# Four-part expert weights issued ahead of the next pair's queries and mask rows on SyncE's DMA queue

## The reference, cut to what matters

```
x = x + einsum('bct,bcd->bdt', x, w0[cond])      # layer 0: a 64x64 matrix chosen per sequence
x = x + attention(x, Wq, Wk, Wv, Wo, k_blocks, v_blocks, block_tables, kv_lens)
                                                 # layer 1: 8 heads, 4 kv groups, window of 256 keys
x = x + einsum('bsi,bio->bso', x, W[id]) + b[id] # layer 2: one of 16 experts, 512x512, per sequence
x = x + x W3^T + scaling * (x A^T) B^T           # layer 3: dense, with one of 8 adapters of rank 16
```

## Time and profile before

| | us |
|---|---|
| median of 3 runs (lowest, highest) | 1223.86 (1220.88, 1235.68) |
| the profiled execution's own time | 1219.34 |
| span of the profiled execution | 1217.5 |
| mean granted clock of TensorE | 0.955 of full |
| busy: TensorE / VectorE / GpSimd / ScalarE | 1075.5 / 652.0 / 529.0 / 485.2 |
| moved by DMA | 187.90 MB, mean 154 GB/s |

### The profile page before, as it was taken

The page is one execution under the profiler, slowest core; times in us unless marked ns, Lnnn a source line. Parts: engine busy times, 40 slices in busy tenths (PEclk is TensorE's granted clock), DMA queues, the critical chain, the costliest instruction groups (busy, mean ns, idle before and its releaser), DMA issues.

```text
span 1217.5 us, 23807 instructions
## 1 busy us (share of the span) xinstructions
PE 1075.5 (88%) x6602; PEld 726.5 (60%) x6602; DVE 652.0 (54%) x1924; ACT 485.2 (40%) x1295; POOL 529.0 (43%) x598
## 2 busy tenths in 40 slices
PE   1999899999626898999999999999999999999997
PEld 0766677887413565556666565665566655656555
DVE  5789886337713454545545455554555555454542
ACT  3344343224413343444444444344444444444440
POOL 2344443324554545545445445444454445444400
PEclk9999998779857898999999999999999999999998
DMA  3334343334234554665555665556565566554530
GB/s 104 107 119 141 118 149 104 107 115 154 104 110 149 170 170 142 189 200 193 161 165 178 188 208 167 167 176 179 193 192 170 159 192 200 186 163 159 175 135 18
DMA packets 90376, 187.90 MB, mean 154 GB/s; under 512 B 30386, under 2 KB 39218, under 8 KB 82150
## 3 DMA queue, kind: packets, MB, share of 16 engines
q1 hardware_dynamic: 59622, 143.35, 34.7%
q0 software_dynamic: 30720, 44.15, 13.9%
HBM read 186.83 MB, written 33.56 MB: 181 GB/s over the span
## 4 chain that ended last, share of the span: by engine, by line
PE 55%; issue 4%; DVE 4%; ACT 2%; DMA 1%; POOL 0%; ACTq 0%; DVEq 0%; POOLq 0%
PE bank L85 18%; PE bank L1246 9%; PE bank L1216 8%; PE bank L1195 7%; PE bank L1203 5%; PE bank L1182 4%; PE bank L1172 2%; DVE SM L1081 2%; ACT PT L1003 1%; DMA KV<-kv_scratch,idxs 1%; PE bank L1235 1%; DVE XAL L1075 1%; DVE XAM L1124 0%; DVE XAH L1129 0%; DMA KV<-in_pool,idxs 0%
## 5 line engine op out<-in xcount | busy, mean ns | idle before, releaser
L940 POOL DMA_INDIRECT KV<-kv_scratch,idxs x192 | 190.5, 992 | 287.5 <-DMA KV<-in_pool,idxs 248.5
L1081 DVE CUSTOM_DVE_ANT_0 SM<-bank,FM 128x336 f32<-128x336 f32 x256 | 130.1, 508 | 253.6 <-PE bank L1195 198.5
L930 POOL DMA_INDIRECT KV<-in_pool,idxs x192 | 192.5, 1003 | 136.7 <-PE bank L1216 68.8
L1003 ACT ACTIVATE PT<-bank 112x384 f32<-112x384 f32 x256 | 112.3, 489 | 263.8 <-PE bank L1203 188.3
L1012 ACT ACTIVATE PR<-SM,nb 128x336 f32<-128x336 f32 x256 | 145.1, 576 | 0.6 <-DVE nb L1085 0.6
L1216 PE MATMUL bank<-PT,KV 112*64 112x128 f32 x1536 | 111.4, 280 | 28.7 <-ACT PT L1003 24.3
L1216 PEld LDWEIGHTS bank<-PT,KV 112*64 112x64 f32 x1536 | 84.3, 137 | 78.6 <-issue 44.6
L1003 ACT ACTIVATE KT<-bank 128x336 f32<-128x336 f32 x128 | 57.7, 451 | 175.3 <-PE bank L1182 168.5
L1246 PE MATMUL bank<-W,XT 128*64 128x512 f32 x512 | 123.7, 604 | 0.9 <-issue 0.7
L85 PE MATMUL bank<-wqh,XTH 128*128 128x512 f32 x256 | 107.0, 418 | 12.2 <-DVE XTL L470 11.8
L673 POOL TENSOR_TENSOR RT<-RT,SW 128x384 f32<-128x384 f32 x32 | 32.4, 1012 | 188.4 <-DVE SW L479 188.4
(11 more groups left out here) (166 smaller groups left out, 1946.2 us busy)
## 6 DMA issues: line engine op xcount, KB each, us to landing
W<-in_w SPq DMA_DIRECT2D x64, 1024.0 KB
FM<-mask SPq DMA_DIRECT2D x64, 168.0 KB
X<-in_x SPq DMA_DIRECT2D x32, 256.0 KB, 2.9
x_scratch<-X SPq DMA_DIRECT2D x32, 256.0 KB, 2.0
kv_scratch<-KVR SPq DMA_DIRECT2D x32, 256.0 KB, 2.6
qt_scratch<-QT SPq DMA_DIRECT2D x32, 256.0 KB, 2.9
QB<-qt_scratch SPq DMA_DIRECT2D x32, 256.0 KB
XB<-x_scratch SPq DMA_DIRECT2D x32, 256.0 KB
```

The source lines that it names most:

```text
L930: pool.indirect_dma_start(out=KV[k][:, c, :], out_offset=None, in_=t["pool"], in_offset=bass.IndirectOffsetOnAxis(ap=idxs[k][:, c:c + 1], ...
L940: pool.indirect_dma_start(out=KV[k][:, c, :], out_offset=None, in_=kv_d, in_offset=bass.IndirectOffsetOnAxis(ap=idxs[k][:, NCH + c:NCH + c ...
L1003: return nc.scalar.activation(dst, src, ACT.Copy)
L1081: v.tensor_tensor_reduce(out=SM[u % 2][:, :], in0=bank[u % 2][:, 0:SPAN], in1=FM[k][:, :], scale=1.0, scalar=-3e38, op0=ALU.add, op1=ALU.m ...
```

## The change

The function `weights` of SyncE now takes a list of parts and a step. Each part is a quarter of a sequence's expert weights (128 partitions x 512 values, 256 KB) with a DMA of its own, so a pair has eight DMAs of 256 KB where it had two of 1 MB, and TensorE waits for 64 counts of the semaphore instead of 16. Ahead of each two parts SyncE waits for a score step of pair p. All weights of pair p are issued behind the XB1 load of body p, and the queries and mask rows of pair p+1 behind them all. Another semaphore, `s_pass_sp`, is only counted up.

```diff
-                    def weights(b):
-                        e = sp.value_load(eid[0:1, bass.ds(p * 2 + b, 1)], min_val=0, max_val=E - 1)
-                        wait(sp, s_l2, p - 1)
-                        sp.dma_start(W2[pr.par][b][:, :], w2_v[bass.ds(e, 1)]).then_inc(s_w2in[pr.par][b], 16)
-
+                    def weights(b, parts, step):
+                        if parts[0] == 0:
+                            regs[b] = sp.value_load(eid[0:1, bass.ds(p * 2 + b, 1)], min_val=0, max_val=E - 1)
+                            wait_all(sp, s_pass_sp, (s_l2, p - 1))
+                        wait_all(sp, s_pass_sp, (s_s, at(p, 8, 2 * step + 1)))
+                        for k in parts:
+                            cols = slice(k * D, (k + 1) * D)
+                            sp.dma_start(W2[pr.par][b][:, cols], w2_v[bass.ds(regs[b], 1), :, cols]
+                                         ).then_inc(s_w2in[pr.par][b], 16)
+
+                    regs = [None, None]
 
                     if isinstance(p, int) and p == 0:
                         sp.wait_ge(s_new[1], 16 * NCH)
-                    if attention:
-                        weights(0)
                     if adapted:
                         store(p - 2)
                     if not attention:
                         return
                     wait(sp, s_x2, p)
                     sp.dma_start(XB1[:, :], x1_d[bass.ds(p, 1)]).then_inc(s_x1in, 16)
+                    weights(0, (0, 1), 0)
+                    weights(0, (2, 3), 1)
+                    weights(1, (0, 1), 2)
+                    weights(1, (2, 3), 3)
                     if not last_pair(pr):
                         queries(pr.move(1))
                         windows(pr.move(1))
-                    weights(1)
...
                             if k == 0:
-                                pe.wait_ge(s_w2in[pr.par][half], at(pr.i, 16, 15))
+                                pe.wait_ge(s_w2in[pr.par][half], at(pr.i, 16 * KC, 16 * KC - 1))
```

More of the change, by code:

```diff
@@ L140, in build @@
         s_pass_dve = sem("dve_passed")
+        s_pass_sp = sem("sp_passed")
         s_prep = sem("prep_step")
```

## The result

The changed kernel took 1505.6 us (median of 4, 1488.8 to 1513.1) against 1223.1 for the kernel before (median of 4): a ratio of 1.227, 95% interval 1.214 to 1.240. The ratio is taken from fast executions alone, for the changed kernel three with a mean of 1500.0 us, while its profiled execution, 1513.1 us, is the one slow one. It is much slower, as forecast, and 70 us slower than the 1436 us that were named; the time lies just above the range.

What follows compares the result with a forecast made beforehand. TensorE's own work was taken to bound the steady part. To 1219.3 us the forecast added 30 stalls of 5.1 us plus 2.6 us of lost clock (+231) and took off 14 won back: 1436 us, range 1290 to 1500.

Steps and rivals of the forecast that it cites:

- The bound: Steady part of phase B: only TensorE's own work sets the pace, about 25.6 us a pair.
- The waits pace nothing: SyncE's four waits on scores: counts are there when SyncE arrives; cost fractions of a microsecond.
- QB's issue at 7.6 us behind XB1: SyncE's queue: eight parts take 6.9 us to issue, QB follows 0.64 behind, at 724.6.
- The queue ahead of QB: SyncE's in-order queue: XB1 and 2.10 MB of weights, beside GpSimd's gather, delay QB to 730.0; stall 5.1 us.
- the second stretch: After four us at 235 GB/s with the gather, the other 2.37 MB take 7.0 us at 341 GB/s.
- the upper end: QB's transfer at 267 GB/s over the whole burst: 12.4 us, landing at 731.3, stall 6.4 us.
- The clock: TensorE behind each stall: granted clock falls to 0.5, 2.6 us lost each time; ends 0 and 5.2.
- What is won: First stretch of phase B: stalls for keys won back, -14 us, no less than 0 and no more than 17.
- Case (d): Steady bodies: stall as forecast, clock low longer, 30 x (5.1 + 5.2) - 14: 1514 us; chance 0.08.
- (a): Start of TensorE's body: QB in time, no stall, only the first stretch's gain left: 1205 us; chance 0.09.
- (b): SyncE's queue: weights through as fast as issued, stall 2.6 us; 1361 us with clock's fall, 1283 without; chance 0.16.
- (c): SyncE's queue: parts don't overlap, 2.9 us each, stall about 18 us, about 1840 us; chance 0.02.

Runs made afterwards that it cites:

- first execution: The changed kernel's profiled execution in the first measurement, against the kernel before: 1513.1 us, the one slow execution; median of the four 1505.6 us.
- chip A: Chip where the changed kernel was run again, unaltered, beside some follow-up runs: 1468.8 us, ratio 1.186 to the kernel before there.
- rerun: The changed kernel run again with no edit, beside the follow-up runs: 1468.8 us, ratio 1.186 to the kernel before.
- filled kernel: The changed kernel with 24 unread matmuls ahead of TensorE's wait for QB, from pair 2 on: 1372.7 us, ratio 1.109 to the kernel before.
- run with few bytes: The changed kernel with each of the eight weight DMAs loading only a quarter of its part (64 KB): 1271.3 us, ratio 1.028 to the kernel before.
- parts alone: The kernel before with each 1 MB weight load cut into four 256 KB DMAs at its old place: 1228.2 us, ratio 0.995.

## Why the prediction was right in kind and short in size

Two terms of the sum were too small, and nearly equal parts of the miss come from each: the stall, "a stall of 5.1 us", measured 6.2 us in the profiled execution, and the clock, "2.6 us lost for each stall", measured 3.7. The causes named for both were right.

- **The bound** was read rightly: in the steady part only TensorE counts, so moved transfers could only add stalls.
- **The waits pace nothing**: shown, by taking them out (1.192 against 1.186, and the same 13.3 us from XB1 to the scores).
- **QB's issue at 7.6 us behind XB1**: 8.7 in the first execution, 6.9 on chip A. It mattered little, since the bytes decided: issuing 3.5 us earlier took 0.6 off the stall.
- **The queue ahead of QB**: right in mechanism. QB ahead of the weights: no wait; a quarter of their bytes ahead: 2.0 us, half: 2.6, all: 5.4. The size was 5.1; measured 5.4 on chip A and 6.2 in the profiled execution. The step that failed is the rate of the second stretch. For the first four us 235 GB/s was right (226 and 241 in the first execution in two bodies at the same distance behind XB1), but what followed ran at 309 and 263, not at the 341 I took from a two-microsecond window of the earlier trace rows. Over the whole stretch from XB1 to the scores it was 262 in the body shown and 232 to 262 in bodies 5 to 26, so the 267 of the upper end, a stall of 6.4, was the better guide. 31 stalls of 6.2 are 192 us where my term was 30 x 5.1 = 153. Why the first execution was fed more slowly than the rerun (240 to 274 GB/s) is open.
- **The clock**: this is the term that failed most against its own size. I took the 2.6 us that the stretch from keys to scores loses. But the stall is at the head of the body, and the stretch that runs at 1.2 GHz begins with the scores, a turning and the values, ahead of the one I measured. From these scores to the next step the loss is near 1.5 us behind some stalls and 4.9 behind others: 115 us in the first execution, 3.7 each, and 97 in the rerun, 3.1 each, where filling the stall won 96. It was 78 in the sum. What decides which of the two prices a stall has is open.
- **What is won** was put at 14 us. The profiled execution was 1513.1 - 1219.3 = 294 us longer; the stalls and the clock together make 192 + 115 = 307, so some 13 us came back, and the waits for keys behind 400 us are gone, as forecast. On chip A the filled kernel has 30 bodies longer by about 5.6 us (31.0 against 25.4), 168 us, and is only 133 us slower than the kernel before, so some 34 us came back. That the kernel before has more stalls for keys to lose there would fit, but it has no profile on that chip.
- Together: the two terms are 307 us where 231 stood, which is 76 of the 77 us between 1436 and the 1513.1 of the profiled execution: 39 from the stall and 37 from the clock. Pairs came every 35.8 us in the mean of the steady part, where 33 was forecast. The 1513.1 is the slowest of the four executions, and how the terms split in the others isn't known. Case (d), the stall with a dearer clock, given 0.08, has 1514 us, but by luck: its stall of 5.1 was too short and its clock's 5.2 too dear. The range's upper end had one stall's upper bound with the clock's middle value; with both upper bounds, 11.6 us for each stall, it would have held the time.
- **The rivals**: (a) fell with QB never in time; (b) would have needed an empty queue, and the run with few bytes shows such a stall, 2.0 us, when the bytes are taken away; (c) fell: parts alone cost nothing, and the eight parts and QB were all in 13.3 us behind XB1. The fixed cost of about 2.0 us that the Trainium skill (DMA: Bandwidth & Descriptors) gives for a DMA stands there in the section Anatomy of one DMA — SWDGE (gpsimd) path, as a fit for DMAs issued by GpSimd, and by it eight parts would be 16 us dearer than their bytes, not 14. No such cost shows on these queued loads of SyncE: parts alone had a ratio of 0.995.

## What to carry to other kernels

On an in-order DMA queue, ask of each load not when it is needed but what is queued ahead of it, in bytes: a small load that the next step begins with goes ahead of large ones that have twenty microseconds to spare. A pacing wait only paces if its event still lies ahead when the issuing engine gets there; put behind the queries and tied to the next pair's scores, the same eight parts came out at 0.980 of the kernel before. And a stall on TensorE costs more than its length when the clock falls in it, here 3.1 to 3.7 us on top of 5.4 to 6.2: count the work that follows, from the stall's place on.

## What the runs showed of the hardware

- Stalls of one length had two prices. Of two stalls of 5.6 and 5.0 us in one execution the clock was back at full within the next 8.2 us (mean 0.80) behind the first, and stayed at 0.50 for all of the next 11.8 us behind the second. Of the rerun's 31 stalls 16 cost 1.1 to 1.6 us and 15 cost 4.9 to 5.0 us up to the next scores, with nothing between. Where stalls were 2.0 us, the clock's mean in the steady part was 0.97.
- The same kernels differed between the first measurement and the later ones on chips A to C: before 1223 and 1238 to 1240 us, the changed kernel 1506 and 1469. SyncE's eight issues took 6.9 us in one trace and 5.1 in the other. So a ratio measured in one place (1.227, 1.186) is not the other's; whether the chip is the cause wasn't tried.
- Cutting the weights into 256 KB parts at their old places cost nothing (0.995). Behind the queries, the gather beside the weights waited 6.4 us with parts and 7.0 with whole loads, in one trace each, on different chips.
- On SyncE's queue a 256 KB load waited for the bytes ahead of it: the scores that need it began 13.3 us behind the head of the burst with all 2.1 MB of weights ahead, 10.4 with half and 9.8 with a quarter, in the means of bodies 5 to 30 on chips A and B. With a quarter ahead it was SyncE's issuing that counted.
